# One core, attention and a 4-bit feed-forward in one kernel: attention steps without loops, another slot for Silu, later maxima, earlier first heads

## The chip, the cores and the metric

One core of one Trainium2 chip. The metric is the time of one execution on the device, in microseconds (us), the median of several runs.

## The reference

The input x has 2 x 1024 tokens of 1024 values. The output is x + attention(xn) * silu(ffn(xn)), with xn the layer-normalised x.

```python
q = rope((xn @ wq).reshape(b, s, 32, 32)); k = rope((xn @ wk).reshape(b, s, 8, 32)); v = ...
k, v = repeat(k, 4, axis=2), repeat(v, 4, axis=2)
attn = softmax(q k^T / sqrt(32) + causal mask)
s = (attn @ v) @ wo
w_gu, w_d = dequant(...)                 # sc[g] * (4-bit weight - (4-bit zero + 1))
gate, up = split(xn @ w_gu)              # 2752 columns each
g = silu((silu(gate) * up) @ w_d)
return x + s * g
```

## The kernel before

Values are carried as a high and a low 16-bit half, so a product is three matmuls. The kernel has three blocks, and every engine has its own instruction stream in each; between them all engines meet.

**Block one** (`project_qkv`) normalises x, turns it into xT, and computes q, k and v in four chunks of 512 tokens (tc), ten output tiles each (j), with rope; the results go to DRAM scratch. SyncE issues all DMAs in program order: at each (tc, j) it stores one tile (`store_qk`, L319 for q and L322 for k). At tc == 3, j == 8 (L349) it also waits until the table selection on VectorE is finished (`selecting`) and loads the q, k and v of the first two head groups for block two: `load_heads` (L92, L93) and `load_values` (L98), 14 DMAs. The block ends on SyncE with a wait for all stores (L359, L360).

**Block two** (`attend_and_expand`) does two things side by side. Attention runs over 64 heads, one per step; the feed-forward's gate and up products run over 88 units (22 tiles of 128 hidden columns by 4 token chunks), one per step. A step has 8 slots, i = 0 to 7, and each engine's `step` function says what it does in each slot:

- TensorE: scores of the causal row t = ORDER[i] (L970, L973; one or two chunks of up to 512 columns, into two banks `sc_ps` in turn), rebuilding of 4-bit weights (`rebuild`, L1010 and L1015, slots 1 and 5, for t >= 2 also 3 and 7), maxima (L948, L952), the outputs of the head before (L994 to L998), and 6 matmuls of gate (slots 0 to 3) or up (slots 4 to 7) at L1047.
- ScalarE: exp of the scores (L1079), copies of sums, high halves of rebuilt weights (L1098, L1103), and in slot 5 the Silu of the gate (`gated`, L1120). Silu and exp need different activation tables, and an ACT_TABLE_LOAD stands before each change.
- VectorE: the reduce of each maxima (L1167), rebuilding (L1185 or L1190, L1195, L1200), h = silu * up (L1244).
- POOL: the low halves of exps (L1286), of weights (L1296, L1299) and of the hidden tile (L1308).
- SyncE: the shift row (L840), stores of the hidden tile (L848) and of down weights (L856), refills.

The softmax shift of a head is the row maximum, computed ahead. For each pair of heads TensorE computes 12 pieces of scores again (`MAXIMA`), for both heads side by side in `mx_ps`, two banks wide; VectorE reduces each and the next piece waits for that (`mx_taken`). After the last, VectorE takes a minimum and transposes (L1170, L1175), and `send_shift` on SyncE writes the result as one more row under q with four small DMAs (L840); the pair's scores wait for these. The pieces are spread over the slots by `maxima_at`: `LEAD = 6` puts a pair's last piece 11 slots and more before its first scores, and a slot in which slot - LEAD is 3 modulo 4 has no piece (slots 1 and 5).

The steps are numbered -4 to 89. Before step 0, steps -4 to -1 rebuild the first gate and up weights and do the first maxima; no scores run yet. `steps` writes -4 to 7 and 56 to 89 straight, and steps 8 to 55 are a loop (`Fori`, L821) of 6 turns of 8 steps on each engine.

**Block three** (`finish`) does the output projection and the down product.

Of the kernel before, what the change touches and what calls it, by code (L numbers as in the profile page):

```python
# [7 lines left out]
ALU = mybir.AluOpType  # L8
ACT = mybir.ActivationFunctionType
AX_X = mybir.AxisListType.X  # L10
F32 = mybir.dt.float32
# [5 lines left out]
P = 128  # L17
# [37 lines left out]
def at(m, u, off, unroll=2):  # L55

    k = u + off
    return m + k // unroll, k % unroll
# [108 lines left out]
def project_qkv(nc, x, wq, wk, wv, rope, q_d, k_d, v_d, xT, ident, identb, maskb, qT, kT, qk_loaded, vn, v_loaded,  # L167
# [13 lines left out]
    with ExitStack() as ctx:  # L181
# [92 lines left out]
        def _(sp):  # L274
# [62 lines left out]
            for e in range(NCH * CT):  # L337
                tc, j = e // CT, e % CT
                load_tables(e)
                if tc == 0 and j in (0, 2):  # L340
                    load_w(4 + j // 2)
                if j % 2 == 1 and j // 2 < CHT:
                    n = tc * CHT + j // 2 + 2 + CHT
                    if n < TT:
                        load_x(n)
                if j == CT - 1 and tc + 1 < NCH:
                    for i in range(CHT):
                        store_v((tc + 1) * CHT + i)
                if tc == 3 and j == 8:  # L349
                    sp.wait_ge(selecting, 4)  # L350
                    for u in range(2):
                        sp.wait_ge(qk_stored[u], 32 * CT)
                        sp.wait_ge(v_stored[u], 16 * ST // 2)
                    for g in range(2):
                        load_heads(sp, q_d, k_d, qT, kT, qk_loaded, g, g)
                        load_values(sp, v_d, vn, v_loaded, g, g)
                store_qk(e)
# [333 lines left out]
def attend_and_expand(nc, q_d, k_d, v_d, o_d, identb, maskb, qT, kT, qk_loaded, vn, v_loaded, probs, p_lo, o, o_stored,  # L691
# [9 lines left out]
    SC = [(t, max(c, t * P), c + BANK) for t in ORDER for c in range(t * P // BANK * BANK, S, BANK)]  # L701
    NC = len(SC)
    SC_BANKS = 2
    LEAD = 6
    MAXIMA = [(7, 0), (7, 1), (0, 0), (6, 0), (6, 1), (1, 0), (5, 0), (2, 0), (5, 1), (4, 0), (3, 0), (4, 1)]
    NM = len(MAXIMA)
    WIDE = BANK // VW
# [6 lines left out]
    with ExitStack() as ctx:  # L714
# [15 lines left out]
        sc_ps = [ctx.enter_context(nc.psum_tensor(f"sc_ps{i}", [P, BANK], F32)) for i in range(SC_BANKS)]  # L730
        mx_ps = ctx.enter_context(nc.psum_tensor("mx_ps", [P, 2, BANK], F32))
        o_ps = ctx.enter_context(nc.psum_tensor("o_ps", [P, BANK], F32))
        gate_ps = ctx.enter_context(nc.psum_tensor("gate_ps", [P, BANK], F32))
        up_ps = ctx.enter_context(nc.psum_tensor("up_ps", [P, BANK], F32))
        sz_ps = ctx.enter_context(nc.psum_tensor("sz_ps", [P, 2, HALF], F32))

        ones_set = sem("ones_set_a")
# [38 lines left out]
        def pair(m, r):  # L776
            return R // 2 * m + r // 2
# [22 lines left out]
        def maxima_at(m, r, i):  # L800
# [7 lines left out]
            m, r = at(m, r - r % 2, ahead, R)  # L808
            return (m, r, slot // 4 * 3 + slot % 4) if exists(m, r) else None

        def chunks_to(t):

            return max(i + 1 for i, c in enumerate(SC) if c[0] == t)

        def steps(eng, step):

            for r in range(-TC, 0):
                step(*at(0, 0, r, R))
            for r in range(R):
                step(0, r)  # L820
            with eng.Fori(1, NH // R - 1) as m:  # L821
                for r in range(R):
                    step(m, r)
            for k in range((NH // R - 1) * R, NU + 2):
                step(*at(0, 0, k, R))

        def count(m, r):
# [3 lines left out]
        def _(sp):  # L831
# [84 lines left out]
                    load_attended(sp, o_d, a, a_loaded, 0, 0, k - KT)  # L916

            def step(m, r):
                if r % 2:
                    send_shift(*at(m, r, 1, R))  # L920
                store_hidden(*at(m, r, -1, R))
                store_down(*at(m, r, -1, R))
                refill_values(*at(m, r, -2, R))
                store_sums(*at(m, r, -3, R))
                refill_weights(m, r)
                prefetch(m, r)
                refill_heads(m, r)

            sp.wait_ge(zeros_set, 1)
            steps(sp, step)  # L930
            for q in range(2):
                sp.wait_ge(ht_stored[q], 16 * NU // 2)
                sp.wait_ge(wd_stored[q], 16 * 2 * FTILES)
# [2 lines left out]
        def _(pe):  # L936
            def maxima(m, r, k):

                u, q, n = r // REP, r % REP, NM * pair(m, r) + k
                t, c = MAXIMA[k]  # L940
                if k == 0 and q == 0:
                    pe.wait_ge(qk_loaded[u], 96 * (m + 1))
                if not isinstance(m, int) or n >= 1:
                    pe.wait_ge(mx_taken, n)
                first, end = c * BANK, min((c + 1) * BANK, (t + 1) * P)
                diagonal = end == (t + 1) * P
                for e in range(2):
                    last = pe.matmul(mx_ps[:, e, 0:end - first], qT[0:STACK, u, q + e, t * P:(t + 1) * P],  # L948
                                     kT[0:STACK, u, first:end], start=True, stop=not diagonal)
                if diagonal:  # L950
                    for e in range(2):
                        last = pe.matmul(mx_ps[:, e, t * P - first:end - first], identb[:, :], maskb[:, :],  # L952
                                         start=False, stop=True)
                last.then_inc(mx_ready, 1)

# [107 lines left out]
                        outputs(*at(m, r, -1, R), i)  # L1063
                    gate_up(m, r, i)

            steps(pe, step)

        @block.scalar
        def _(act):
# [70 lines left out]
            def step(m, r):  # L1140
                for i in range(ST):
                    exps(m, r, i)
                    if i == 0:
                        copy_sums(*at(m, r, -2, R))
                    if i == 1:
                        highs(*at(m, r, -1, R), 7)
                    if i == 2:
                        rounded(*at(m, r, -1, R))
                    if i in (3, 5, 7):
                        highs(m, r, i - 2)  # L1150
                    if i == 5:
                        gated(m, r)
                wo_high(m, r)

            steps(act, step)

        @block.vector
        def _(dve):
            def maxima(m, r, k):
                n, p = pair(m, r), r // 2 % 2  # L1160
                t, c = MAXIMA[k]
                width = min((c + 1) * BANK, (t + 1) * P) - c * BANK
                dve.wait_ge(mx_ready, NM * n + k + 1)
                if k == 0 and (not isinstance(m, int) or n >= 1):
                    dve.wait_ge(shift_turned, n)
                to = shift[:, p, :, t] if width + c * BANK == (t + 1) * P else part[:, p, :, t - BANK // P]
                dve.tensor_reduce(to, mx_ps[:, :, 0:width], AX_X, ALU.max, negate=True).then_inc(mx_taken, 1)  # L1167
                if k == NM - 1:
                    dve.wait_ge(mx_taken, NM * (n + 1))
                    dve.tensor_tensor(shift[:, p, :, BANK // P:ST], shift[:, p, :, BANK // P:ST], part[:, p, :, :],  # L1170
                                      ALU.min).then_inc(shift_done, 1)
                    dve.wait_ge(shift_done, n + 1)
                    if not isinstance(m, int) or n >= 2:
                        dve.wait_ge(shift_loaded[p], 64 * ((R // 4) * m + r // 4))
                    dve.transpose(shT[:, p, :], shift[:, :, :, :].rearrange("p a h t -> p (a h t)")  # L1175
                                  ).then_inc(shift_turned, 1)
# [96 lines left out]
                last = dve.memset(o[:, :, WIDE, q * VW + VH:(q + 1) * VW], 0.0)  # L1273
            last.then_inc(zeros_set, 1)
            dve.wait_ge(shift_set, 1)
            steps(dve, step)

        @block.gpsimd
        def _(pool):
# [39 lines left out]
                low(m, r, 3)  # L1319
                lows(m, r, 5)  # L1320

            steps(pool, step)


def load_attended(eng, o_d, a, a_loaded, b, m, u):
# [490 lines left out]
```

## Time and profile before

| | us |
|---|---|
| median of 3 runs | 2522.42 |
| lowest and highest run | 2519.57, 2523.61 |
| profiled execution | 2521.81 |
| its span | 2520.3 |
| busy in the span: PE (TensorE) | 2357.8 (94%) |
| DVE (VectorE) | 1204.8 (48%) |
| ACT (ScalarE) | 889.2 (35%) |
| POOL | 1013.6 (40%) |
| DMA, mean share of 16 engines | 25% |
| granted TensorE clock, mean (1 is full speed) | 0.977 |
| block two's first scores | 375.7 |
| block two's last TensorE matmul | 1842.4 |

All times in the trace count from the start of the span. Idle time of an engine is put down to what released it; idle time without a releaser is called "issue". A matmul's end is modelled, so neighbouring matmuls overlap in the rows, and starts are the safer reading.

### The profile page before, as it was taken

The page shows a single profiled execution, that of the slowest core. Times are in us where ns is not written, and L with a number is a line of the kernel's source. Part 1 is how long each engine was busy: PE and PEld are TensorE (multiplying, and loading weights), DVE is VectorE, ACT ScalarE, POOL GpSimd, SP SyncE. Part 2 cuts the span into 40 slices and gives each one's busy share as a digit, 9 for nine tenths or more (in the row PEclk, how much of TensorE's full clock was granted, in tenths as well). Part 3 has the DMA queues.
Part 4 walks back from the last instruction along what each step waited for, and adds up shares of the span by engine and source line. Part 5 has one row for each costly group of instructions (what it writes and reads, how often), then busy time and mean ns, then how long its engine had stood idle before and what let it go on. Part 6 is the DMA issues. An engine that isn't in the chain of part 4 may idle for free. (4 is left out here: it accounts for less than half of the span.)

```text
span 2520.3 us, 45248 instructions
## 1 busy us (share of the span) xinstructions
PE 2357.8 (94%) x16808; PEld 1223.2 (49%) x16808; DVE 1204.8 (48%) x2164; ACT 889.2 (35%) x1665; POOL 1013.6 (40%) x748
## 2 busy tenths in 40 slices
PE   6899939999999999999999999999969999999999
PEld 3555415555555555555555555444434444444443
DVE  4688455666666565655666665555331212121100
ACT  3222105555555555555555555322210111010100
POOL 2555315666556565665656656433200000001000
PEclk9999959999999999999999999999989999999999
DMA  5332210222212122212222222233262313132220
GB/s 159 100 95 63 52 47 10 73 51 69 65 49 60 52 73 63 56 51 66 58 68 58 57 60 55 64 97 104 55 250 86 136 57 112 56 112 79 72 79 17
DMA packets 229150, 188.15 MB, mean 75 GB/s; under 512 B 121617, under 2 KB 200954, under 8 KB 228544
## 3 DMA queue, kind: packets, MB, share of 16 engines
q1 hardware_dynamic: 228928, 185.21, 25.0%
q8 instruction: 137, 2.24, 0.4%
q14 instruction: 85, 0.70, 0.1%
HBM read 113.17 MB, written 71.86 MB: 73 GB/s over the span
## 5 line engine op out<-in xcount | busy, mean ns | idle before, releaser
L1286 POOL TENSOR_TENSOR room<-room 128x1152 f16<-128x1152 f32 x256 | 539.9, 2109 | 477.8 <-ACT room L1079 477.8
L1079 ACT ACTIVATE room<-sc_ps 128x512 f32<-128x512 f32 (+3 forms) x768 | 348.9, 489 | 542.5 <-PE sc_ps L973 520.4
L1047 PE MATMUL gate_ps<-xT,wg 128*128 128x512 f16 x2064 | 500.9, 381 | 0.7 <-ACT h L1120 0.7
L1047 PE MATMUL up_ps<-xT,wg 128*128 128x512 f16 x2064 | 495.3, 378 | 1.0 <-ACT h L1120 1.0
L1492 PE MATMUL dn_ps<-xT,hT_in 128*128 128x512 f16 x1536 | 337.3, 380 | 0.0
L1167 DVE TENSOR_REDUCE shift<-mx_ps 128x2 f16<-128x1024 f32 (+3 forms) x256 | 211.9, 828 | 195.1 <-PE mx_ps L952 194.6
L1677 POOL TENSOR_TENSOR room<-room 128x512 f32<-128x512 f32 x32 | 52.8, 1652 | 617.7 <-DVE room L1638 617.7
L970 PE MATMUL sc_ps<-arena 97*128 97x512 f16 (+3 forms) x768 | 233.8, 330 | 49.3 <-ACT room L1079 34.2
L1047 PEld LDWEIGHTS gate_ps<-xT,wg 128*128 128x128 f16 x2064 | 184.7, 97 | 186.5 <-issue 5.4
L1047 PEld LDWEIGHTS up_ps<-xT,wg 128*128 128x128 f16 x2064 | 181.2, 97 | 183.8 <-ACT h L1120 1.8
L1492 PEld LDWEIGHTS dn_ps<-xT,hT_in 128*128 128x128 f16 x1536 | 148.8, 98 | 181.6 <-issue 7.5
L1638 DVE TENSOR_TENSOR room<-room 128x512 f32<-128x512 f32 x32 | 24.0, 754 | 428.7 <-ACT room L1566 428.6
L1167 DVE TENSOR_REDUCE part<-mx_ps 128x2 f16<-128x1024 f32 x128 | 157.0, 1227 | 150.3 <-PE mx_ps L948 150.2
L647 PE MATMUL qk_ps<-xT,w 128*128 128x512 f16 x960 | 211.9, 382 | 6.2 <-DVE w L497 6.2
L948 PE MATMUL mx_ps<-arena 96*128 96x512 f16 (+3 forms) x768 | 195.6, 337 | 19.0 <-DVE part L1167 9.6
L1195 DVE TENSOR_TENSOR stock<-stock,sz_ps 128x256 f32<-128x256 uint32 (+2 forms) x264 | 110.1, 417 | 172.1 <-PE sz_ps L1010 132.9
L998 PE MATMUL o_ps<-arena,room 128*128 128x33 f16 x2304 | 192.0, 178 | 0.0
L1483 PE MATMUL out_ps<-room,stock 128*128 128x512 f16 x768 | 171.2, 383 | 9.1 <-DVE stock L1631 7.9
L998 PEld LDWEIGHTS o_ps<-arena,room 128*128 128x128 f16 x2304 | 157.7, 96 | 23.4 <-issue 0.3
L1566 ACT ACTIVATE room<-dn_ps 128x512 f32<-128x512 f32 x32 | 19.1, 597 | 422.8 <-PE dn_ps L1492 422.5
L1296 POOL TENSOR_TENSOR wg<-wf,wg 128x256 f16<-128x256 f32 (+1 forms) x176 | 121.4, 690 | 115.7 <-ACT wg L1098 115.7
L994 PE MATMUL o_ps<-arena,room 128*128 128x65 f16 x1792 | 160.8, 191 | 0.0
(119 smaller groups left out, 3126.1 us busy)
## 6 DMA issues: line engine op xcount, KB each, us to landing
hidden_scratch<-hT SPq DMA_DIRECT2D x84, 256.0 KB, 3.1
hT_in<-hidden_scratch SPq DMA_DIRECT2D x16, 1344.0 KB, 5.9
o_scratch<-room SPq DMA_DIRECT2D x16, 1040.0 KB, 6.0
room<-o_scratch SPq DMA_DIRECT2D x16, 1040.0 KB, 8.2
arena<-q_scratch SPq DMA_DIRECT2D x48, 256.0 KB, 3.7
stock<-in_qw_d SPq DMA_DIRECT2D x42, 256.0 KB
down_scratch<-wd SPq DMA_DIRECT2D x84, 128.0 KB, 2.5
xin<-in_x SPq DMA_DIRECT2D x16, 512.0 KB, 3.8
```

Of the source, the lines that this page charges most:

```text
L647: last = pe.matmul(qk_ps[e % QB][:, :], w[:, wp, s, j * P:(j + 1) * P], xT[:, xp, s, tc * BANK:(tc + 1) * BANK], start=(s == 0 and k == 0) ...
L948: last = pe.matmul(mx_ps[:, e, 0:end - first], qT[0:STACK, u, q + e, t * P:(t + 1) * P], kT[0:STACK, u, first:end], start=True, stop=not d ...
L970: last = pe.matmul(bank[:, 0:e - c], kT[0:STACK + 1, u, t * P:(t + 1) * P], qT[0:STACK + 1, u, q, c:e], start=True, stop=(c > t * P))
L994: pe.matmul(o_ps[:, c:c + VW], hi, vn[:, u, k, :], start=first, stop=False)
L998: last = pe.matmul(o_ps[:, c:c + VH], lo, vn[:, u, k, 0:VH], start=False, stop=final)
L1047: last = pe.matmul(to[:, :], wg[:, u, wp, s, cols], xT[:, xp, s, tokens], start=(s == 0 and k == 0), stop=(s == KT - 1 and k == 2))
L1079: act.activation(probs[:, r % 2, START[t] + c:START[t] + e], sc_ps[n % SC_BANKS][:, 0:e - c], ACT.Exp, scale=float(1.0 / np.sqrt(HD))).the ...
L1167: dve.tensor_reduce(to, mx_ps[:, :, 0:width], AX_X, ALU.max, negate=True).then_inc(mx_taken, 1)
L1286: pool.tensor_tensor(p_lo[:, r % 2, c], probs[:, r % 2, c], p_hi[:, r % 2, c], ALU.subtract).then_inc(lo_done, 1)
L1296: pool.tensor_tensor(wg[:, u, 1, n, 0:2 * wt], wf[:, p, 0:2 * wt], wg[:, u, 0, n, 0:2 * wt], ALU.subtract).then_inc(lo_half, 1)
L1483: last = pe.matmul(out_ps[:, cols], aT[:, u, xp, s, :], w[:, wp, s, cols], start=(s == 0 and k == 0), stop=(s == KT - 1 and k == 2))
L1492: last = pe.matmul(dn_ps[u][:, half, :], hT[0:wt, u, hp, j, :], src[0:wt, wp, half * BANK:(half + 1) * BANK], start=(j == 0 and k == 0), s ...
```

## The change

There are five edits.

1. SyncE loads the first heads at j == 2 of the last chunk and not at j == 8.
2. `steps` runs from -4 to 89 in one straight row, without a loop, on all engines.
3. ScalarE does the Silu (`gated`) in slot 4.
4. `LEAD` is 12. A pair's pieces of maxima come 6 slots later; the slots without a piece are 3 and 7. The first pair's pieces go to `mx_ps` and `gu_ps` in turn, where `gu_ps` is the gate bank and the up bank as one tensor, and a piece waits for the reduce of the one before the last.
5. In `step` of SyncE, `send_shift` comes behind the stores of the hidden tile and of the down weights.

```diff
-                if tc == 3 and j == 8:
+                if tc == 3 and j == 2:
                     sp.wait_ge(selecting, 4)
...
-    LEAD = 6
+    LEAD = 12
...
-        gate_ps = ctx.enter_context(nc.psum_tensor("gate_ps", [P, BANK], F32))
-        up_ps = ctx.enter_context(nc.psum_tensor("up_ps", [P, BANK], F32))
+        gu_ps = ctx.enter_context(nc.psum_tensor("gu_ps", [P, 2, BANK], F32))
+        gate_ps, up_ps = gu_ps[:, 0, :], gu_ps[:, 1, :]
...
+        def maxima_banks(m, r, k):
+
+            return gu_ps if pair(m, r) == 0 and k % 2 else mx_ps
+
...
-        def steps(eng, step):
-
-            for r in range(-TC, 0):
-                step(*at(0, 0, r, R))
-            for r in range(R):
-                step(0, r)
-            with eng.Fori(1, NH // R - 1) as m:
-                for r in range(R):
-                    step(m, r)
-            for k in range((NH // R - 1) * R, NU + 2):
+        def steps(step):
+
+            for k in range(-TC, NU + 2):
                 step(*at(0, 0, k, R))
...
             def step(m, r):
+                store_hidden(*at(m, r, -1, R))
+                store_down(*at(m, r, -1, R))
                 if r % 2:
                     send_shift(*at(m, r, 1, R))
-                store_hidden(*at(m, r, -1, R))
-                store_down(*at(m, r, -1, R))
...
-                if not isinstance(m, int) or n >= 1:
+                to = maxima_banks(m, r, k)
+                if pair(m, r) == 0 and k >= 2:
+                    pe.wait_ge(mx_taken, n - 1)
+                if pair(m, r) >= 1:
                     pe.wait_ge(mx_taken, n)
...
-                    if i == 5:
+                    if i == 4:
                         gated(m, r)
...
-                dve.tensor_reduce(to, mx_ps[:, :, 0:width], AX_X, ALU.max, negate=True).then_inc(mx_taken, 1)
+                dve.tensor_reduce(to, maxima_banks(m, r, k)[:, :, 0:width], AX_X, ALU.max, negate=True).then_inc(mx_taken, 1)
```

On ScalarE, slots 3 to 7 of step 0, before (sc_ps rows are exps, gate_ps is the Silu's source):

```order
L1079 ACTIVATE room<-sc_ps 128x384
L1079 ACTIVATE room<-sc_ps 128x256
L1079 ACTIVATE room<-sc_ps 128x512
L1120 ACT_TABLE_LOAD
L1120 ACTIVATE h<-gate_ps 128x512
L1079 ACT_TABLE_LOAD
L1079 ACTIVATE room<-sc_ps 128x512
L1079 ACTIVATE room<-sc_ps 128x128
```

The same place in the changed kernel:

```order
L1079 ACTIVATE room<-sc_ps 128x384
L1120 ACT_TABLE_LOAD
L1120 ACTIVATE h<-gu_ps 128x512
L1079 ACT_TABLE_LOAD
L1079 ACTIVATE room<-sc_ps 128x256
L1079 ACTIVATE room<-sc_ps 128x512 x2
L1079 ACTIVATE room<-sc_ps 128x128
L1079 ACTIVATE room<-sc_ps 128x512
```

The Silu with its two table loads now stands between the exp of slot 4 (384 columns) and the two of slot 5 (256 and 512), and no longer between slots 5 and 6.

On TensorE, the start of block two, before (sz_ps rows are rebuilds, mx_ps rows are pieces of maxima with their masks at L952):

```order
L1010 MATMUL sz_ps<-stock,sel_gu 128x512 x2
L948 MATMUL mx_ps<-arena 128x512 x4
L952 MATMUL mx_ps<-maskb,identb 128x128 x2
L948 MATMUL mx_ps<-arena 128x128 x2
L952 MATMUL mx_ps<-maskb,identb 128x128 x2
L1010 MATMUL sz_ps<-stock,sel_gu 128x512
L948 MATMUL mx_ps<-arena 128x512 x2
L948 MATMUL mx_ps<-arena 128x384 x2
L952 MATMUL mx_ps<-maskb,identb 128x128 x2
```

The same place in the changed kernel:

```order
L1010 MATMUL sz_ps<-stock,sel_gu 128x512 x3
L948 MATMUL mx_ps<-arena 128x512 x2
L1010 MATMUL sz_ps<-stock,sel_gu 128x512
L948 MATMUL gu_ps<-arena 128x512 x2
L952 MATMUL gu_ps<-maskb,identb 128x128 x2
L948 MATMUL mx_ps<-arena 128x128 x2
L952 MATMUL mx_ps<-maskb,identb 128x128 x2
L948 MATMUL gu_ps<-arena 128x512 x2
L1010 MATMUL sz_ps<-stock,sel_gu 128x512
L948 MATMUL mx_ps<-arena 128x384 x2
```

Three rebuilds, not two, now stand before the first piece, the pieces change banks, and a rebuild falls beside a piece where before it stood in a slot of its own. Before the first scores there were 20 pieces, and there are 15 now: the five last ones stand behind the first scores.

On TensorE, slots 4 and 5 of step 0, before (L970 and L973 are scores and their mask, L1047 the product of up):

```order
L970 MATMUL sc_ps<-arena 128x384
L973 MATMUL sc_ps<-identb,maskb 128x128
L948 MATMUL mx_ps<-arena 128x128 x2
L952 MATMUL mx_ps<-maskb,identb 128x128 x2
L1047 MATMUL up_ps<-xT,wg 128x512 x6
L970 MATMUL sc_ps<-arena 128x256
L973 MATMUL sc_ps<-identb,maskb 128x128
L970 MATMUL sc_ps<-arena 128x512
L1010 MATMUL sz_ps<-stock,sel_gu 128x512
L1047 MATMUL up_ps<-xT,wg 128x512 x6
```

The same two slots in the changed kernel (gu_ps at L1047 is the up bank):

```order
L970 MATMUL sc_ps<-arena 128x384
L973 MATMUL sc_ps<-identb,maskb 128x128
L948 MATMUL mx_ps<-arena 128x512 x2
L1047 MATMUL gu_ps<-xT,wg 128x512 x6
L970 MATMUL sc_ps<-arena 128x256
L973 MATMUL sc_ps<-identb,maskb 128x128
L970 MATMUL sc_ps<-arena 128x512
L1010 MATMUL sz_ps<-stock,sel_gu 128x512
L948 MATMUL mx_ps<-arena 128x384 x2
L952 MATMUL mx_ps<-maskb,identb 128x128 x2
L1047 MATMUL gu_ps<-xT,wg 128x512 x6
```

Slot 5 has a piece of maxima now, and slot 4 a wider one.

## Rows read from the trace of the kernel before

**Rows 1.** Busy time by stretch, the attention stage; busy us (x instructions) of each engine

```profile
core 0: us, PE busy (x) PEld busy (x) DVE busy (x) ACT busy (x) POOL busy (x), PEclk, DMA share, GB/s
...
400.00:1520.00 1120.00, 1072.14 (x9988) 607.17 (x9987) 686.05 (x1252) 615.98 (x1224) 672.97 (x468) 0.99 0.22 59
```

**Rows 2.** Waits of TensorE: line, releaser: us in total, times, longest us

```profile
PE sc_ps L970 <- ACT room L1079: 34.2, 64, 1.1
...
PE sc_ps L970 <- issue: 15.1, 5, 3.3
```

**Rows 3.** Timeline of TensorE at the marks, and busy time after a turn

```profile
600.19 0.39 PE L970 MATMUL sc_ps<-arena 97*128 97x512 f16 x1 [0.64 <-ACT room L1079]
...
618.74 0.39 PE L970 MATMUL sc_ps<-arena 97*128 97x512 f16 x1 [0.34 <-ACT room L1079]
...
674.98 0.39 PE L970 MATMUL sc_ps<-arena 97*128 97x512 f16 x1 [0.63 <-ACT room L1079]
...
698.24 0.39 PE L970 MATMUL sc_ps<-arena 97*128 97x512 f16 x1 [0.33 <-ACT room L1079]
...
835.00:845.00 10.00, 9.71 (x60) 4.68 (x61) 3.56 (x6) 3.10 (x8) 3.84 (x3) 0.66 0.20 55
```

**Rows 4.** Timeline of ScalarE and TensorE, slots 4 to 7 of one step

```profile
1110.66 0.38 ACT L1079 ACTIVATE room<-sc_ps 128x256 f32<-128x256 f32 x1 [1.36 <-PE sc_ps L973]
...
1115.65 0.49 ACT L1079 ACTIVATE room<-sc_ps 128x384 f32<-128x384 f32 x1 [1.63 <-PE sc_ps L973]
...
1118.73 1.28 ACT L1120 ACT_TABLE_LOAD   x1
1120.02 0.60 ACT L1120 ACTIVATE h<-gate_ps 128x512 f32<-128x512 f32 x1
...
1115.23 0.33 PE L970 MATMUL sc_ps<-arena 97*128 97x384 f16 x1
...
1119.42 0.38 PE L970 MATMUL sc_ps<-arena 97*128 97x512 f16 x1
...
1121.67 0.22 PE L970 MATMUL sc_ps<-arena 97*128 97x128 f16 x1
...
1122.58 0.39 PE L970 MATMUL sc_ps<-arena 97*128 97x512 f16 x1 [0.64 <-ACT room L1079]
```

**Rows 5.** Timeline of TensorE, one piece of maxima inside a step

```profile
1142.09 0.49 PE L948 MATMUL mx_ps<-arena 96*128 96x384 f16 x2
1142.42 0.28 PE L952 MATMUL mx_ps<-maskb,identb 128*128 128x128 bf16 x2
```

**Rows 6.** End of block one: timelines of POOL, SyncE, TensorE, a stretch, a wait of SyncE

```profile
317.51 2.26 POOL L388 TENSOR_TENSOR ql<-rot,qh 128x512 f16<-128x512 f32 x2 [1.29 <-ACT qh L439]
...
322.38 0.80 SPq L322 DMA_DIRECT2D k_scratch<-ql  x1
...
326.00:328.00 2.00, 0.00 (x0) 0.00 (x0) 0.00 (x0) 0.00 (x0) 0.00 (x0) 0.50 0.27 96
...
SPq L359 <- DMA k_scratch<-ql: 7.7, 1, 7.7
...
331.50 0.62 PE L1010 MATMUL sz_ps<-stock,sel_gu 72*128 72x512 bf16 x1 [17.39 <-PEq L181]
```

**Rows 7.** Before the first scores: timelines, and DVE busy on L1167 alone in a stretch

```profile
336.92 1.22 DVE L1167 TENSOR_REDUCE part<-mx_ps 128x2 f16<-128x1024 f32 x1
...
341.76 0.28 DVE L1185 TENSOR_SCALAR stock<-stock 128x256 uint32<-128x256 uint32 x1
...
342.98 1.23 DVE L1167 TENSOR_REDUCE part<-mx_ps 128x2 f16<-128x1024 f32 x1
...
331.50:360.20 28.70, 11.55 (x12) 0.50 0.00 0
...
360.56 2.52 SPq L840 DMA_DIRECT2D arena<-shT  x4
...
375.70 0.31 PE L970 MATMUL sc_ps<-arena 97*128 97x128 f16 x1
```

**Rows 8.** Timeline of SyncE, the hidden store in an odd step

```profile
1132.55 0.71 SPq L848 DMA_DIRECT2D hidden_scratch<-hT  x1
```

More of the change, by code:

```diff
@@ L929, in _ @@
             sp.wait_ge(zeros_set, 1)
-            steps(sp, step)
+            steps(step)
             for q in range(2):
@@ L947, in maxima @@
                 for e in range(2):
-                    last = pe.matmul(mx_ps[:, e, 0:end - first], qT[0:STACK, u, q + e, t * P:(t + 1) * P],
+                    last = pe.matmul(to[:, e, 0:end - first], qT[0:STACK, u, q + e, t * P:(t + 1) * P],
                                      kT[0:STACK, u, first:end], start=True, stop=not diagonal)
@@ L951, in maxima @@
                     for e in range(2):
-                        last = pe.matmul(mx_ps[:, e, t * P - first:end - first], identb[:, :], maskb[:, :],
+                        last = pe.matmul(to[:, e, t * P - first:end - first], identb[:, :], maskb[:, :],
                                          start=False, stop=True)
@@ L1064, in step @@
                     gate_up(m, r, i)
-            steps(pe, step)
+            steps(step)
         @block.scalar
@@ L1150, in step @@
                         highs(m, r, i - 2)
-                    if i == 5:
+                    if i == 4:
                         gated(m, r)
                 wo_high(m, r)
-            steps(act, step)
+            steps(step)
         @block.vector
@@ L1275, in _ @@
             dve.wait_ge(shift_set, 1)
-            steps(dve, step)
+            steps(step)
         @block.gpsimd
@@ L1320, in step @@
                 lows(m, r, 5)
-            steps(pool, step)
+            steps(step)
 def load_attended(eng, o_d, a, a_loaded, b, m, u):
```

## The prediction

> **What bounds the kernel now.** I read the busy time of each engine by stages first: in the 1120 us of the attention stage TensorE is busy for 1072, VectorE for 686, POOL for 673, ScalarE for 616 [rows 1]. So what counts is where TensorE stands idle, and why. Its waits come next [rows 2]: in the attention stage one wait is met once per head, 64 times, for an exp of ScalarE, and one comes five times with no releaser ("issue"). Then I read TensorE in time order around three places: a turn of the loop [rows 3], slots 4 to 7 of one step [rows 4], and the time between the projection's last matmul and the first scores [rows 6, 7]. The change touches all three and nothing after the attention stage, so everything is summed over them. The profiled execution took 2521.8 us, 0.6 below the median of the runs; the sum is made against it.
>
> **Loops written out.** The mark is the second score matmul of slot 7, one per step. From the last step of a group of four to the first of the next it comes after 18.55 us inside the loop (600.19 to 618.74), but after 23.26 where the loop turns (674.98 to 698.24) [rows 3]: 4.7 lost. The same reading at the other four turns gives 6.7, 6.6, 4.8 and 4.6, together 27.4; the two long ones hold a stretch whose granted clock is 0.66, that is partly 1.2 GHz, right after the pause (835 to 845). 3.0 of each is the "issue" wait itself [rows 2], the rest is the pipeline of the engines filling again. Steps 0 to 7 and 56 to 87 are straight code already, and TensorE shows no issue wait there, so I take the written-out steps to have none: **-27.4**. Bounds: 0 (straight code pauses as often) and 27.4. The Trainium skill, Advanced Engine Details and Errata, section Control Flow Timing, gives 51 ns for a branch and 108 ns for a compare with one. By that five turns would be worth 0.8 us, and the sum would end at 2459; the row at the turn shows thirty times as much, so I take the row.
>
> **Silu in slot 4, and what the later maxima do for it.** A step has 8 slots; score chunks go to two banks in turn, so the chunk in slot 6 needs the exp of slot 5's first chunk, and slot 7's second chunk needs slot 6's. Before, ScalarE does slot 5's exps, then table load 1.28, Silu 0.60, table load 1.28, then slot 6's exp; TensorE waits in slot 7: 0.64 idle in the row at 1122.58 [rows 4]. The first chunk of the slot began at 1121.67 and the second would follow 0.12 behind it, so 0.79 is lost; each of the 64 idle times hides some 0.15 more. 34.2 [rows 2] + 64 x 0.15 = 44 us in all. Now the Silu comes after slot 4's exp. That exp starts 0.42 after slot 4 does (1115.65 against 1115.23) and takes 0.49; with 1.28 + 0.60 + 1.28 and the exp of 256 columns, 0.38, and small gaps, the bank is free 4.5 to 4.6 us after slot 4 began. Slot 6 began 4.19 after slot 4 (1119.42), so alone the move would only turn a stall of 0.5 to 0.8 into one of 0.35 to 0.4. But the maxima move too: they now leave out slots 3 and 7, and lie in slot 5, where they were left out before. A pair of 384 columns takes 0.33 to its masks and these 0.11 [rows 5]; slot 5 gets 0.44 to 0.54 longer, slot 4 gets 0.1 to 0.2 longer. Slot 6 is then due 4.8 to 4.9 after slot 4: about 0.2 behind the bank. Slot 7's second chunk needs an exp that ends 0.8 before it. So no stall is left in steps 0 to 60; in the last three no maxima run, and 0.6 to 0.75 each stays, 2.0. **-42.4**. Bounds: 17 (a stall of 0.4 to 0.45 in every step) and 44. Here a rule of the Trainium skill speaks against the change. In the row the Silu starts 0.01 after the 1.28 of the load. The page ScalarE: Activation LUTs, section What ACT_TABLE_LOAD costs, counts 1.38 us of drain on top of each load; by it slot 6 would wait 2.5 us in every step and the kernel end above 2570. The row has no such drain.
>
> The other engines have room: VectorE is at 61% and POOL at 60% of the steps' time [rows 1]. In slots 1 and 5 VectorE now has a reduce (up to 1.23) ahead of the rebuild's 1.2 [rows 7]; TensorE's next maxima need only the reduce, with 0.2 to 0.4 to spare. I cost this at nothing; if that cover goes, TensorE waits for the bank of the maxima.
>
> **Maxima later.** Five of the second pair's maxima, which ran before the first scores, now run beside them, where TensorE has no idle time: 5 x 0.42 by the same row [rows 5]: **+2.1**. What else moves is the time left for the shift row: the last maxima of a pair are in slot 2 of the odd step before its scores. SyncE now first issues that step's hidden store (1132.55, 10 us behind the mark of the step before at 1122.58) [rows 4, 8], then two stores of down weights, 1.4, then four transfers, 2.5 [rows 7], landing some 2 later: at 1139. A step of 18.3 after that mark is the step's own, and the next scores are 2.6 behind it: at 1143.5, 4 us to spare. That is the reason for the new order on SyncE, and it hides everything. The heads' buffers are asked for 6 slots later than before, which only helps.
>
> **Heads loaded sooner.** Before, SyncE issues 14 loads between 314.0 and 320.5, ahead of the last four stores of k; the last is issued at 323.2 and the end of the block waits 7.7 us for it, to 330.9; block two starts 0.6 later [rows 6]. Now the loads are issued at about 283, when their guard (the table selection, finished on VectorE at 276.0) is open. The last low half is ready at 319.8 (317.51 + 2.26), so the last store goes out by 320.5. The four stores are 512 KB, and the queue moved such stores at 96 GB/s at 326 to 328: 5.5 us from about 318.6, done at 324.5. **-6.3**. Bounds: 2.7 (issue time alone) and 8. The loads fall among other stores of the last chunk; a store of step 32 is 4 us late, and has two steps of 5.2 to catch up.
>
> **The stretch before the first scores.** Before: 44.2 us (331.50 to 375.70), 20 maxima one after the other in one bank pair, three in 6.06 us, since each waits for the reduce before it, at a granted clock of 0.50. Now 12 + 3. Three rebuilds come first: the second ends on VectorE at +5.4 (336.92), a third adds 1.9. With two bank pairs TensorE works ahead, and VectorE bounds it: 12 reduces 11.6, four rebuilds of 1.2, minimum and transpose 0.4 [rows 7], gaps 0.5: the shift row is ready at +24.6. Four transfers and their landing: 4.3. First scores at **+29.0**; three maxima of the next pair run beside that and end at the same time. **-15.2**. Bounds: 10 (only the five maxima saved, 2.0 each) and 18 (the third rebuild hidden).
>
> **Sum**: 2521.8 - 27.4 - 42.4 + 2.1 - 6.3 - 15.2 = **2432.6 us**. With the small bounds of the last two terms, and some lost tenths per step, this case spans 2424 to 2443.
>
> **Rivals.**
> - *The stall moves to slot 6.* My margin is 0.2 us in 4.8, made of five durations; if the exp is released late, TensorE waits 0.2 to 0.45 in each of 61 steps: 12 to 27 back, 2445 to 2460, with 0.35 at 2454. For it: the margin, and that nothing in this trace shows maxima and rebuild in one slot. Against: both estimates come from steady rows. 18%.
> - *Straight code pauses too.* The loop's pause might be the price of reaching new code, and 48 written-out steps reach new code all the time: 27 back, 2459. Against: steps 0 to 7 and 56 on lie outside the loop and show none. 8%.
> - *Slower: the shift row comes late.* The scores of a pair now wait for a chain through SyncE that has 4 us to spare. If POOL's low half of the hidden tile came at the step's end and not in its slot 3, the transfers would be 8 us later and TensorE would wait 4 for each of 31 pairs: 2433 + 124 = 2557. It decides from 7 us of lateness (4 spare, and 89 / 31 = 2.9 more). Against: the row of the hidden store at 1132.55, and POOL idle for 40% of the stage [rows 1]. 2%.
> - *Slower: each table change costs 2.7.* Slot 6 waits 2.5 in 61 steps, 2433 + 152 = 2585, as a drain behind each load would have it; the row of the Silu speaks against it. 1%.
> - *The change doesn't do what it says*: both large terms come back in part and it ends within 0.2% of before. 1%.
>
> **How the numbers follow.** The forecast case has 70%. The range reaches from its low end over the first rival's middle, 2424 to 2456; outside lie the second rival, the slow ones and the tails. 0.2% (5 us) is about what a measurement can tell from no change. Faster by more: 0.96; within: 0.01; slower: 0.03.
>
> **What would show it.** Right: no "issue" wait on the score matmuls; the wait of score matmuls for ScalarE down from 34 us in 64 times to under 4 in a few; the first scores at about 354; the step mark of four steps 72.2 us apart (74.8 before); the wait for the last store about 4 us. Wrong: a wait of the slot 6 chunk for ScalarE (0.2 or more per step), a wait of mx_ps matmuls for VectorE inside the steps, a wait for the DMA of shT, or issue gaps at regular distances.

## The result, and the profile after

| | us |
|---|---|
| before, median | 2522.5 |
| changed kernel, median of 4 runs | 2477.2 (2473.1 to 2479.1) |
| ratio, 95% interval | 0.982 (0.9803 to 0.9837) |
| profiled execution, its span | 2473.1, 2471.4 |
| forecast | 2432.6 (2424 to 2456) |

The kernel is 45 us faster, where 89 were forecast, and it ends above the range. Engine by engine, first TensorE and VectorE on the page of the changed kernel (share of the span, instructions):

```profile
PE 2349.5 (95%) x16808; PEld 1214.4 (49%) x16808; DVE 1320.0 (53%) x2164; ACT 890.5 (36%) x1665; POOL 1021.7 (41%) x748
```

VectorE is busy for 1320.0 us with the work that took 1204.8 before: 115 us more. Then TensorE's waits, columns as in [rows 2]:

```profile
PE mx_ps L948 <- DVE part L1167: 28.1, 31, 1.3
```

This line leads the list. Neither a wait of the score matmuls for ScalarE (34.2 before) nor an "issue" wait on them (15.1 before) [rows 2] is in the attention steps any more, except 1.5 us in the last three. A wait for VectorE has come in their place. The same stretch as [rows 1]:

```profile
400.00:1520.00 1120.00, 1091.61 (x10213) 612.33 (x10210) 818.65 (x1284) 633.48 (x1257) 695.82 (x479) 1.00 0.22 60
```

The marks of the first scores, in time order on TensorE, and SyncE's wait for the last store, which answer to [rows 6, 7]:

```profile
325.79 0.62 PE L1010 MATMUL sz_ps<-stock,sel_gu 72*128 72x512 bf16 x1 [11.86 <-PEq L181]
...
354.59 0.31 PE L970 MATMUL sc_ps<-arena 97*128 97x128 f16 x1
```

```profile
SPq L359 <- DMA k_scratch<-ql: 5.0, 1, 5.0
```

Block two begins 5.7 us sooner (331.50 to 325.79), and from there to the first scores it takes 28.8 and not 44.2. These two terms came as forecast (6.3 and 15.2). Then the step mark of [rows 3], the second score matmul of slot 7, from the last step of one group of four to that of the next:

```profile
651.82 0.38 PE L970 MATMUL sc_ps<-arena 97*128 97x512 f16 x1
...
726.58 0.38 PE L970 MATMUL sc_ps<-arena 97*128 97x512 f16 x1
```

74.76 us, where 72.2 were forecast, and 74.79 lay between the marks before. The steps gained nothing. Slot by slot, from the starts of the score matmuls and against the same slots in experiment 6, where no wait for VectorE is left: slot 1 of a group's first step takes 4.72 and not 2.99, slot 5 of its third step 3.38 and not 2.70, and slot 5 of its fourth and second 0.13 and 0.04 too much: 2.58 us for each group. The first of the 16 groups lacks slot 1's wait, so it is 40 us in all. Two falls of the granted clock, 1.7 us each, come on top (last section).

**Why VectorE is late.** The operations of VectorE between 400 and 1520 us, grouped by line (count, busy us, mean ns, idle before). Before:

```profile
L1190 DVE TENSOR_SCALAR stock<-stock,lanes 128x256 uint32<-128x256 uint32 x59 | 74.6, 1264 | 0.5
L1195 DVE TENSOR_TENSOR stock<-stock,sz_ps 128x256 f32<-128x256 uint32 x175 | 73.7, 421 | 68.0 <-PE sz_ps L1010 64.0 <-DVE stock L1185 0.2
...
L1185 DVE TENSOR_SCALAR stock<-stock 128x256 uint32<-128x256 uint32 x116 | 37.4, 322 | 0.4
...
L140 DVE TENSOR_SCALAR stock<-stock 72x256 bf16<-72x256 f32 x15 | 4.2, 281 | 0.0
L156 DVE CAST stock<-stock 8x256 bf16<-8x256 uint32 x14 | 3.9, 281 | 0.5
```

After:

```profile
L1185 DVE TENSOR_SCALAR stock<-stock 128x256 uint32<-128x256 uint32 x120 | 91.9, 766 | 0.5
L1195 DVE TENSOR_TENSOR stock<-stock,sz_ps 128x256 f32<-128x256 uint32 x180 | 75.8, 421 | 9.1 <-PE sz_ps L1010 1.6
...
L156 DVE CAST stock<-stock 8x256 bf16<-8x256 uint32 x15 | 32.6, 2170 | 0.5
L140 DVE TENSOR_SCALAR stock<-stock 72x256 bf16<-72x256 f32 x15 | 31.0, 2068 | 0.0
...
L1190 DVE TENSOR_SCALAR stock<-stock,lanes 128x256 uint32<-128x256 uint32 x60 | 22.0, 366 | 0.5
```

L140 to L156 build the next tile's table of scales (`build_table`, called by `next_table` in four pieces: slots 3 and 6 of the third and fourth step of a group). A cast of 8 x 256 values takes 2.17 us instead of 0.28. L1195, which has one input in PSUM (the memory that matmuls write to; `stock` and `room` lie in SBUF), keeps its 421 ns. And L1190 was already at 1264 ns before, though L1185, with the same 128 x 256 values, took 322. The timelines of VectorE, POOL and TensorE in the changed kernel, from a fourth step into the next group, show why:

```profile
650.94 2.03 DVE L153 TENSOR_SCALAR stock<-stock 8x32 uint32<-8x32 uint32 x8
653.00 2.17 DVE L156 CAST stock<-stock 8x256 bf16<-8x256 uint32 x1
...
656.86 1.22 DVE L1167 TENSOR_REDUCE part<-mx_ps 128x2 f16<-128x1024 f32 x1
```

```profile
649.74 2.11 POOL L1286 TENSOR_TENSOR room<-room 128x1152 f16<-128x1152 f32 x1 [3.06 <-ACT room L1079]
651.80 0.69 POOL L1299 TENSOR_TENSOR wd<-wf,wd 128x256 f16<-128x256 f32 x1
652.92 2.11 POOL L1286 TENSOR_TENSOR room<-room 128x1152 f16<-128x1152 f32 x1 [0.43 <-ACT room L1079]
```

```profile
658.14 0.50 PE L948 MATMUL mx_ps<-arena 96*128 96x384 f16 x2 [1.30 <-DVE part L1167]
```

L156 starts 0.08 us after one of POOL's low halves of the exps (L1286) and ends 0.14 after it (655.17 against 655.03). All 15 L156 and all 15 L140 of this window end 0.13 to 0.15 us after the L1286 beside which they began, and so did all 59 L1190 in the trace before. The eight small L153 ahead of L156 take 2.03 together (0.77 before), since the L1286 of 649.74 holds the first of them, and that pushes L156 into the next L1286. Behind them stand the rebuild, h = silu * up and then the reduce, and for that TensorE waits. The chain of the other stall is the same: L140 at 625.00 beside an L1286 that starts at 624.81, the reduce at 627.80, TensorE's piece at 629.07 with 0.52 idle:

```profile
624.81 2.11 POOL L1286 TENSOR_TENSOR room<-room 128x1152 f16<-128x1152 f32 x1 [0.91 <-ACT room L1079]
```

```profile
625.00 2.07 DVE L140 TENSOR_SCALAR stock<-stock 72x256 bf16<-72x256 f32 x1
...
627.80 1.21 DVE L1167 TENSOR_REDUCE part<-mx_ps 128x2 f16<-128x1024 f32 x1
```

```profile
629.07 0.50 PE L948 MATMUL mx_ps<-arena 96*128 96x384 f16 x2 [0.52 <-DVE part L1167]
```

The Trainium skill, page SBUF — State Buffer, section Who interferes with whom, says what this looks like: VectorE and GpSimd share one pair of SBUF ports as an exclusive lock, casts and `tensor_scalar` can take it, and whoever comes second is blocked for the whole instruction of the first. The rows agree, with 2.17 for 0.28; I had not weighed that section in the prediction.

### The profile page after: what moved, and what is told of

Its sections match the earlier page's. It is cut to its first block and busy times, and to the rows that moved or that the text cites. A ratio compares the mean times of both kernels' runs of the same rounds, so it can differ in the third digit from the quotient of the medians.

```text
span 2471.4 us, 41585 instructions
## 1 busy us (share of the span) xinstructions
PE 2349.5 (95%) x16808; PEld 1214.4 (49%) x16808; DVE 1320.0 (53%) x2164; ACT 890.5 (36%) x1665; POOL 1021.7 (41%) x748
## 5 line engine op out<-in xcount | busy, mean ns | idle before, releaser
L1047 PE MATMUL gu_ps<-xT,wg 128*128 128x512 f16 x4128 | 988.2, 379 | 1.7 <-ACT h L1120 1.7
L1286 POOL TENSOR_TENSOR room<-room 128x1152 f16<-128x1152 f32 x256 | 539.8, 2109 | 403.3 <-ACT room L1079 403.3
L1047 PEld LDWEIGHTS gu_ps<-xT,wg 128*128 128x128 f16 x4128 | 368.0, 97 | 384.2 <-issue 4.5
L1167 DVE TENSOR_REDUCE shift<-mx_ps 128x2 f16<-128x1024 f32 (+2 forms) x252 | 209.0, 829 | 138.1 <-PE mx_ps L952 137.9
L970 PE MATMUL sc_ps<-arena 97*128 97x512 f16 (+3 forms) x768 | 226.0, 328 | 1.6 <-ACT room L1079 1.5
L948 PE MATMUL mx_ps<-arena 96*128 96x512 f16 x756 | 189.7, 332 | 32.7 <-DVE part L1167 28.1
L1167 DVE TENSOR_REDUCE part<-mx_ps 128x2 f16<-128x1024 f32 x126 | 153.5, 1218 | 57.6 <-PE mx_ps L948 57.2
L1195 DVE TENSOR_TENSOR stock<-stock,sz_ps 128x256 f32<-128x256 uint32 (+2 forms) x264 | 110.1, 417 | 106.5 <-PE sz_ps L1010 61.3
L1296 POOL TENSOR_TENSOR wg<-wf,wg 128x256 f16<-128x256 f32 (+1 forms) x176 | 126.8, 721 | 93.2 <-ACT wg L1098 93.1
L647 PEld LDWEIGHTS qk_ps<-xT,w 128*128 128x128 f16 x960 | 94.1, 98 | 118.0 <-issue 9.4
L1308 POOL TENSOR_TENSOR hT<-h,hT 128x512 f16<-128x512 f32 (+1 forms) x88 | 102.0, 1159 | 97.6 <-ACT hT L1130 97.3
```

The costliest lines, as they stand in the source:

```text
L647: last = pe.matmul(qk_ps[e % QB][:, :], w[:, wp, s, j * P:(j + 1) * P], xT[:, xp, s, tc * BANK:(tc + 1) * BANK], start=(s == 0 and k == 0) ...
L948: last = pe.matmul(to[:, e, 0:end - first], qT[0:STACK, u, q + e, t * P:(t + 1) * P], kT[0:STACK, u, first:end], start=True, stop=not diag ...
L970: last = pe.matmul(bank[:, 0:e - c], kT[0:STACK + 1, u, t * P:(t + 1) * P], qT[0:STACK + 1, u, q, c:e], start=True, stop=(c > t * P))
L1047: last = pe.matmul(to[:, :], wg[:, u, wp, s, cols], xT[:, xp, s, tokens], start=(s == 0 and k == 0), stop=(s == KT - 1 and k == 2))
L1167: dve.tensor_reduce(to, maxima_banks(m, r, k)[:, :, 0:width], AX_X, ALU.max, negate=True).then_inc(mx_taken, 1)
L1286: pool.tensor_tensor(p_lo[:, r % 2, c], probs[:, r % 2, c], p_hi[:, r % 2, c], ALU.subtract).then_inc(lo_done, 1)
```

## The experiments

Times are medians; an interval against before is some 4 us to either side.

**1. The loops again.** Theory L: the loops' end brought what was forecast; theory V: VectorE, held by POOL, took back the rest.

```diff
-            for k in range(-TC, NU + 2):
+            for r in range(-TC, 0):
+                step(*at(0, 0, r, R))
+            for r in range(R):
+                step(0, r)
+            with eng.Fori(1, NH // R - 1) as m:
+                for r in range(R):
+                    step(m, r)
+            for k in range((NH // R - 1) * R, NU + 2):
                 step(*at(0, 0, k, R))
```

> The changed kernel with the loop over 48 steps put back, everything else kept. Theory L (each turn of the loop costs what the trace of before shows, 4.6 to 6.7 us): 27 us above the changed kernel, near 2504, with five issue waits of about 3 us on the score matmuls. Rival (straight code has a price of its own that the loop did not have): less than 15 above, near 2490.

The cut leaves out that every engine's call names its engine again and that only straight steps choose the first pair's banks. 2499.7 us, ratio 0.9906 (0.989 to 0.9923): 22.5 slower than the changed kernel. Its waits on the score matmuls show the loop's turn again:

```profile
PE sc_ps L978 <- issue: 11.0, 5, 2.8
```

The end of the loops is worth 22 us of the 27.4 forecast. Between the two profiled executions the five steps at the turns differ by 28.8 us, so the size of this term is known to some 6 us only.

**2. Silu in slot 5 again.**

```diff
-                    if i == 4:
+                    if i == 5:
                         gated(m, r)
```

> The changed kernel with the Silu back in slot 5. With the maxima in slot 5 the chain exps, load, Silu, load, exp ends 5.0 to 5.45 us after slot 5 began, and slot 7's second chunk is due after 4.97: a stall of 0.1 in half of the steps and 0.5 in the others, about 1.2 per four steps, 15 to 20 us, near 2495. Rival (the Silu's slot alone removed all 44 us of the old stall): near 2518.

2466.9 us, ratio 0.9782 (0.9765 to 0.9798): 10 us faster than with slot 4, where the theory had 15 to 20 slower and the rival 41 slower. The stall in the first step's slot 1 is gone (2.99), the one in the third step's slot 5 is not (3.38), and slot 7 waits for ScalarE again, by 0.28 a step on average. By line:

```profile
L1185 DVE TENSOR_SCALAR stock<-stock 128x256 uint32<-128x256 uint32 x121 | 155.7, 1287 | 0.5
L140 DVE TENSOR_SCALAR stock<-stock 72x256 bf16<-72x256 f32 x16 | 33.1, 2068 | 0.0
...
L156 DVE CAST stock<-stock 8x256 bf16<-8x256 uint32 x15 | 4.2, 281 | 0.5
```

So L156 is held because of Silu's slot. With Silu in slot 4 the exps of slot 5 come later, and POOL's third low half of the step with them: in the fourth step of a group it starts 2.1 us before the step mark in the changed kernel (649.74 against 651.82), and 4.4 before it here (647.20 against 651.58), much as in the kernel before (4.1). The fourth starts 1.1 behind the mark in all three. The gap between the two is 3.4 us here, and L153 and L156 run in it; in the changed kernel it is 1.1. L140 is held with Silu in either slot. And L1185 at 1287 ns costs nothing there: VectorE's total is no measure of the loss, its place is.

**3. LEAD = 6 again.**

```diff
-    LEAD = 12
+    LEAD = 6
```

> The changed kernel with LEAD = 6, so the maxima leave slots 1 and 5 free again. Theory: TensorE waits for ScalarE in slot 6, 0.35 us per step (+23), no longer for VectorE in slots 1 and 5 (-41), and the first scores come 11 later, less 2 of the moved maxima: near 2468. If the new wait for VectorE comes from something else than the maxima's slots (the Silu's slot, the straight code), it stays, and the time is near 2509.

2511.5 us, ratio 0.9958 (0.9944 to 0.9972), 43 us above my expectation:

```profile
PE mx_ps L948 <- DVE shift L1167: 36.9, 20, 2.2
PE sc_ps L970 <- ACT room L1079: 16.3, 63, 0.8
```

```profile
L153 DVE TENSOR_SCALAR stock<-stock 8x32 uint32<-8x32 uint32 x120 | 54.0, 531 | 0.0
```

The wait for VectorE did not go; it is in slot 0 of each group's first step but the very first now, 2.19 us in each of 15. L140 is back at 282 ns, so its hold came from the later maxima. Here it is above all the eight L153 that are held, 531 ns each and not 176, with L156 at 689 behind them. Behind nine of the 15 waits the granted clock also fell, at some 1.6 us each: 14 of the 43 us.

**4. POOL's operations made short.** Of the low halves of the exps only the first 128 columns of each are computed, so that POOL's operation takes 0.40 us and not 2.11. The rest stays zero; for that POOL clears the buffer once before its first step, a line that the cut below leaves out. VectorE's work is untouched; what is left out is the rest of the exps' low halves. (An added line makes L1185 and L1286 of the changed kernel L1186 and L1287.)

```diff
-                c = slice(START[tiles[0]] + tiles[0] * P, START[tiles[-1]] + S)
+                c = slice(START[tiles[0]] + tiles[0] * P, START[tiles[0]] + tiles[0] * P + P)
```

> The low halves of the exps on POOL are computed for the first 128 columns of each piece only (the rest stays zero), so POOL's 2.11 us instructions become short; VectorE's own work is the same. Theory P (VectorE's instructions on SBUF are held until POOL's long one ends): L1185, L1156 and L1218 lines fall to 0.3 us, the wait of the maxima matmuls for VectorE in steps 4, 8, 12 and on (1.7 us per four steps) and in slot 5 (0.7) vanishes, near 2435. Rival D (VectorE has too much of its own in front of the reduce): the waits stay, 2470 to 2477.

2438.0 us, ratio 0.9664 (0.9648 to 0.968): 39 faster than the changed kernel.

```profile
L156 DVE CAST stock<-stock 8x256 bf16<-8x256 uint32 x16 | 4.5, 281 | 0.6
```

The wait of the maxima for VectorE is gone from the steps. POOL's long operations are the cause, not the amount of VectorE's work. The 39 us hold a cost of the experiment itself, which shows the hold once more: the clearing keeps POOL busy for 7.78 us, and VectorE's first operation of 128 x 256 values ends 0.14 after it:

```profile
327.56 7.78 POOL L1323 MEMSET room<- 128x9216 f16 x1 [6.18 <-POOLq L181]
...
330.27 5.21 DVE L1186 TENSOR_SCALAR stock<-stock 128x256 uint32<-128x256 uint32 x1
```

From block two's start to the first scores it takes 33.8 us here and not 28.8. Without these 5 us the gain would be 44, an estimate from these two numbers, and that is what experiment 6 measures.

**5. The table pieces in another slot.** Everything is computed; L140 to L156 only stand in slot 4 of a group's second to fourth step, where POOL is mostly idle.

```diff
-                if not unit(m, r) or at_slot not in (3, 6):
+                if not unit(m, r) or at_slot != 4:
...
-                if t < 2 or (isinstance(j, int) and j + 2 >= FTILES):
+                if t < 1 or (isinstance(j, int) and j + 2 >= FTILES):
...
-                piece = 2 * (t - 2) + at_slot // 6
+                for piece in [(0, 1), (2,), (3,)][t - 1]:
```

> The changed kernel, but VectorE builds the pieces of the next scale table (L140 to L156) in slot 4 of the second, third and fourth step of a group of four, where POOL has nothing to do, and not in slots 3 and 6 of the last two. Nothing is left out and no operation gets shorter. Theory of the held instructions (VectorE's work on SBUF waits for the end of POOL's 2.11 us operations): L156, L140 and L149 fall back to 0.3 to 0.4 us, the waits of TensorE for the maxima's bank go, and the time falls by most of the 41 us, to 2440 (2436 to 2448). Rival (VectorE simply has too much to do around slots 1 and 5, wherever the pieces stand): 2470 to 2480, with the pieces still near 2 us or TensorE still waiting 25 us or more for VectorE.

2435.3 us, ratio 0.9661 (0.9645 to 0.9677): 42 faster than the changed kernel, from the place of some dozen small instructions a group. VectorE and TensorE at the same piece of maxima as above, with the step mark:

```profile
639.09 0.28 DVE L156 CAST stock<-stock 8x256 bf16<-8x256 uint32 x1
...
646.22 1.22 DVE L1167 TENSOR_REDUCE part<-mx_ps 128x2 f16<-128x1024 f32 x1
```

```profile
643.38 0.38 PE L970 MATMUL sc_ps<-arena 97*128 97x512 f16 x1
...
647.97 0.49 PE L948 MATMUL mx_ps<-arena 96*128 96x384 f16 x2
```

The reduce starts 2.8 us after the mark (5.0 in the changed kernel), and TensorE's piece 4.6 after it with no idle time (6.3 there). VectorE is hardly less busy between 400 and 1520 us, 805.5 us and not 818.7: other operations are held instead, L1185 for 1091 ns on average, at places where nothing waits for them.

**6. The selection moved too.** Experiment 5, with `select` in slot 4 of a group's first step in place of slot 2 of its second.

```diff
-                if not unit(m, r) or unit(m, r)[2] != 1:
+                if not unit(m, r) or unit(m, r)[2] != 0:
...
-                    if i == 2:
+                    if i == 4:
                         select(m, r)
```

> As the kernel before in this study (table pieces in slot 4), and VectorE's selection of rows (four small operations) also goes from slot 2 of the second step to slot 4 of the first. Held instructions: the four operations lose what they waited for POOL, but no TensorE wait hangs on them, since the second step showed only 0.1 us of delay per step: 0 to 2 us faster than with the table pieces alone. Rival (each held microsecond of VectorE costs, wherever it is): 3 us faster or more.

2433.6 us (2432.0 to 2434.4), ratio 0.9648 (0.9632 to 0.9664). This is the best kernel of the study, 89 us faster than before and 44 faster than the change. The 1.8 us beyond experiment 5 are less than a measurement tells. The step mark:

```profile
644.88 0.38 PE L970 MATMUL sc_ps<-arena 97*128 97x512 f16 x1
...
717.05 0.38 PE L970 MATMUL sc_ps<-arena 97*128 97x512 f16 x1
```

72.17 for four steps: the forecast's 72.2. In experiment 5 it was 72.29 to 72.31.

**7. The loads at j == 8 again**, with `j == 8` in place of `j == 2` in the changed kernel.

> The changed kernel, but the first heads' loads are issued at j == 8 of the last chunk, as in the kernel before. Theory: the loads again stand before the last stores of k and TensorE's idle time at the start of block two goes from 11.9 back to 17.4: 5 to 6.5 us slower than the changed kernel, 2483. Rival: the loads were never what the last store waited for, and the same 512 KB bound the block's end: 0 to 1.5 us.

2480.5 us, ratio 0.9831 (0.9815 to 0.9848). In the trace block two starts 6.6 us later:

```profile
332.35 0.62 PE L1010 MATMUL sz_ps<-stock,sel_gu 72*128 72x512 bf16 x1 [17.09 <-PEq L181]
```

The idle time went from 11.9 back to 17.1 as expected, and SyncE's wait for the last store from 5.0 to the 7.7 of before, so the loads are what that store waited for. The medians differ by 3.3 only, within their uncertainty.

**8. One bank pair for the first maxima.**

```diff
-            return gu_ps if pair(m, r) == 0 and k % 2 else mx_ps
+            return mx_ps
...
-                if pair(m, r) == 0 and k >= 2:
-                    pe.wait_ge(mx_taken, n - 1)
-                if pair(m, r) >= 1:
+                if n >= 1:
                     pe.wait_ge(mx_taken, n)
```

> The changed kernel, but the first pair's maxima all go to one bank pair, each waiting for the reduce before it. Theory: TensorE and VectorE take turns again, about 2.0 us for a piece and not 1.1 to 1.5: first scores 6 to 10 us later (at 361 to 365), 2484 to 2487. Rival: VectorE's reduces and rebuilds bound the stretch in both forms: first scores at 355 to 357, 2478.

2483.0 us, ratio 0.9848 (0.9832 to 0.9865), 5.8 slower than the changed kernel. First scores:

```profile
361.75 0.31 PE L968 MATMUL sc_ps<-arena 97*128 97x128 f16 x1
```

Block two began at 325.33 here, so the stretch takes 36.4 and not 28.8: the second bank pair is worth 7.6 of its 15.4. The rest goes with the fewer pieces and the third rebuild, which no run takes apart.

**9. Only Silu in slot 4, all else as before** (in the kernel before, the edit of experiment 2 backwards).

> The kernel before with one edit: Silu in slot 4 and not 5 (loops, LEAD = 6 and all else as before). Theory: ScalarE's stall of 0.65 in slot 7 turns into one of some 0.45 in slot 6 (11 us back), but POOL's low halves come later and hold VectorE's table pieces, so TensorE waits for the maxima of a step's first slots as in the kernel with LEAD = 6: 25 to 35 us more. Together slower than before: 2535 (2528 to 2548). Rival (the sum of the prediction, where VectorE is free): 5 to 17 us faster than before, 2505 to 2517.

2533.5 us, ratio 1.0036 (1.0023 to 1.005): the move alone makes the kernel 12 us slower.

```profile
PE mx_ps L948 <- DVE shift L1167: 30.9, 20, 2.2
...
PE sc_ps L970 <- ACT room L1079: 10.3, 39, 0.8
```

The wait for ScalarE fell from 34.2 to 10.3, and a wait for VectorE of 30.9 stands above it, where 9.1 stood before. The granted clock fell 12 times in the attention steps, and 3 times before.

**10. LEAD = 6 in the best kernel.**

> The fastest kernel so far (table pieces and selection in slot 4) with LEAD = 6 in place of 12. Theory: without VectorE's waits only the wait of slot 6 for ScalarE is left, 0.45 in 61 steps, 27 us, and the first scores are 6 us later: 2434 + 27 + 4 = 2465 (2458 to 2472); this is what the later maxima hide. Rival (with LEAD = 6 VectorE is late also without the table pieces): 2485 or more, with waits of the maxima for VectorE over 20 us.

2464.0 us, ratio 0.9766 (0.9747 to 0.9784): 30 above the best kernel, and 47 below experiment 3, from which it differs in the place of the table pieces and the selection alone.

```profile
PE sc_ps L970 <- ACT room L1079: 16.2, 63, 0.8
```

Of the waits inside the steps only that of slot 6 for ScalarE is left; four steps take 73.77 and not 72.17, 26 us over 16 groups. The first scores are later too (363.68 against 356.36, of which 0.9 is a later start of block two). So the prediction had this right: the later maxima hide what Silu in slot 4 leaves over.

**11. Silu in slot 5 in the best kernel.**

> The fastest kernel so far (table pieces and selection in slot 4) with Silu in slot 5 in place of 4. Theory: with VectorE out of the way the slot of Silu is worth what slot 7's second chunk waits for ScalarE, 0.2 to 0.4 in 61 steps by the run with Silu in slot 5 (mean 0.27): 17 us slower than with slot 4, 2451 (2446 to 2457). Rival (the slot of Silu acts through POOL and VectorE alone): within 3 us of 2434.

2460.7 us, ratio 0.9754 (0.9734 to 0.9773): 27 slower, not 17. With VectorE out of the way slot 7 waits for ScalarE by 0.2 to 0.5 in each step, 0.40 on average. In experiment 2 part of that had been hidden behind VectorE's stalls (in a group's third step, with its stall in slot 5, the wait is 0.20 there and 0.52 here). So Silu's slot is worth +12 in the kernel before, -27 in the best one, and +10 in the change as made.

**12. Only the table pieces and the selection in slot 4, all else as before.**

> The kernel before with the table pieces and the selection in slot 4, and nothing else. Theory: before, VectorE's held instructions lay where nothing waited for them, so their place gains nothing: 2521 (2517 to 2525), with the waits of TensorE for ScalarE still near 34 us. Rival (the place of the pieces is an improvement of its own, whatever Silu does): 2510 or less.

2523.0 us, ratio 0.9999 (0.999 to 1.0009): nothing.

```profile
PE sc_ps L970 <- ACT room L1079: 34.3, 64, 1.1
```

Nothing waited for them there. In the kernel before, this edit is worth nothing and Silu's slot alone is a loss; with the later maxima, the three bring four steps from 74.79 to 72.17, 42 us over 16 groups. The later maxima alone in the kernel before were not tried.

## Why the prediction was wrong

- **The step that failed** is "The other engines have room: VectorE is at 61% and POOL at 60% of the steps' time", with "I cost this at nothing". It added durations as if an operation takes the same time wherever it stands. The runs show that VectorE's table and rebuild operations from SBUF to SBUF last until the long POOL operation that they meet ends (L140, L156 and L1190 some 0.14 us behind it), and the change moved POOL's third low half (by Silu's slot) and the reduces (by LEAD) so that L153, L156 and L140 meet one just ahead of a reduce that TensorE waits for. That cost 40 us by the slots and 3 by the clock, and 39 (with 5 of its own), 42 and 44 in experiments 4, 5 and 6. The text named the result (TensorE waits for the bank of the maxima) and listed it as a sign, but gave it neither a price nor a chance. It could have been seen: L1190's 1264 ns beside L1185's 322 were in the trace of before, each L1190 ending 0.14 or 0.15 us after an L1286.
- **Loops, -27.4**: right in kind, 22.5 by the medians and 28.8 by the traces. No "issue" wait came back in straight code; that rival fell.
- **Silu and maxima, -42.4**: right for the engines it looked at. The exp of 256 columns starts at 648.79 and takes 0.38, so the bank is free 4.6 us after slot 4 began (644.59). Slot 6 comes 4.8 to 4.9 after slot 4 in the best kernel and 5.1 here; no wait of slot 6 is seen, and that rival fell too. What the term was to give shows only in the best kernel (72.17 a group, before 74.79). Its lower bound of 17 was no bound: in the changed kernel a group gained 0.03, half a microsecond in all. A slip in its sum is small beside that: 44 less 2.0 is 42.0, not 42.4.
- **Heads sooner, -6.3**: 5.7 in the trace, 3.3 by the medians of experiment 7; the wait for the last store is 5.0 where about 4 was forecast (318.6 and 5.5 make 324.1, not 324.5). **The stretch before the first scores, -15.2**: 15.4. The first scores came at 354.59, forecast about 354.
- **The shift row** came in time: no wait for shT's DMA. **The table loads** have no drain: L1120's Silu starts 0.01 after its load's end as before, and 2585 was far off.
- Without the failed step the sum holds: 2432.6 forecast, 2433.6 measured in experiment 6. A match within 1 us is luck, as single terms were off by up to 5 us and the medians are uncertain by some 4.

## What to carry to other kernels

When a change moves work of VectorE or POOL in time, list the operations that lie side by side on the two before and after: an SBUF-to-SBUF operation of 0.3 us took 2.2 there. A group whose mean is several times that of the same shape on another line is the sign of it, even where nothing waits for it yet. And try edits in pairs: Silu's slot alone was +12, the table's place alone 0, and together with the later maxima they gave what the sum had promised.

## What the runs showed of the hardware

How long an operation of VectorE is held is set by when POOL's ends, not by its own size: 8 x 256 values (L156) and 128 x 256 (L1185 of 1.72 at 620.58, beside an L1286 of 2.11 that started at 620.05) both end 0.14 us behind POOL's, and behind the clearing of 7.78 us in experiment 4 the same 128 x 256 took 5.21. The reduces of PSUM (L1167, 1024 columns) kept their 1.21 to 1.23 us through all of it.

A short wait also costs clock. Behind 2 of the 15 waits of 1.30 us for VectorE in the changed kernel, equal to the others, the granted clock fell. Stretches of the changed kernel behind such a wait (columns as in [rows 1]):

```profile
808.00:812.00 4.00, 4.00 (x35) 2.14 (x33) 2.33 (x4) 0.19 (x1) 1.68 (x2) 0.59 0.00 0
812.00:815.00 3.00, 3.00 (x35) 1.81 (x34) 0.70 (x1) 1.66 (x5) 1.16 (x1) 0.98 0.00 0
```

For 4 us TensorE was fully busy near the lower of its two levels, 1.2 GHz, and that step took 21.2 us and not 19.55, 1.7 more than its wait. In experiment 3, with waits of 2.19 us, it fell behind 9 of 15, and those steps took some 1.6 us more than the other six. In the best kernel, where these waits are gone, no step shows it. Why it falls behind some of equal waits and not behind others was not tried.
